# A graph network on one core: another order of the first products, their loads and waits, fewer products of a constant, and a square root moved at the end

## The reference

```python
Xw = X @ Wv + bv
sj, si = Xw @ aw[:d, 0], Xw @ aw[d:, 0]
e = leaky_relu(sj[:, None, :] + si[:, :, None] + ab[0], negative_slope=0.2)
alpha = A * exp(e);  T = alpha / (alpha.sum(-1, keepdims=True) + 1e-12)
H = X @ Wk[0] + bk[0] + (T @ X) @ Wk[1] + bk[1] + (T @ T @ X) @ Wk[2] + bk[2]
x = layernorm(x + relu(H))
x = layernorm(x + adj @ x @ w)
```

## Time and profile before

| what | value |
|---|---|
| median of 3 runs | 272.84 us (272.76 to 273.21) |
| the profiled execution's own time | 273.95 us |
| its span, from the first to the last instruction | 272.1 us |
| around the span | 1.85 us |
| TensorE matmuls (PE) busy | 266.3 us, 98% |
| VectorE (DVE) busy | 216.8 us, 80% |
| ScalarE (ACT) busy | 191.6 us, 70% |
| GpSimd (POOL) busy | 190.3 us, 70% |

### The profile page before, as it was taken

One profiled execution on the slowest core, in us unless ns is written; L12 is line 12 of the kernel. 1 busy time (PEld: TensorE's weight loads), 2 busy tenths in 40 slices (PEclk: granted clock), 3 DMA queues, 4 the chain that ended last, 5 costly groups with the idle time before them and its releaser, 6 DMA issues.

```text
span 272.1 us, 6029 instructions
## 1 busy us (share of the span) xinstructions
PE 266.3 (98%) x1887; PEld 246.6 (91%) x1887; DVE 216.8 (80%) x615; ACT 191.6 (70%) x437; POOL 190.3 (70%) x412
## 2 busy tenths in 40 slices
PE   8999999999999999999999999999999999999992
PEld 3899999999999999999999999999999999999991
DVE  0677788888898888889888888988888888788994
ACT  2688677776667777666777766677766677767874
POOL 2567547788777777877778787777887777657533
PEclk9999999999999999999999999999999999999998
DMA  7858245749584378545764448844883347922214
GB/s 222 292 164 135 30 147 125 81 139 150 150 151 145 58 136 140 165 142 155 126 86 123 146 155 143 150 121 79 133 161 99 117 115 87 135 75 77 79 41 154
DMA packets 28758, 34.91 MB, mean 128 GB/s; under 512 B 7091, under 2 KB 16694, under 8 KB 28726
## 3 DMA queue, kind: packets, MB, share of 16 engines
q1 hardware_dynamic: 28016, 34.12, 56.7%
q10 hardware_dynamic: 710, 0.40, 0.5%
HBM read 26.09 MB, written 8.42 MB: 127 GB/s over the span
## 4 chain that ended last, share of the span: by engine, by line
PE 93%; DVE 2%; DMA 1%; POOL 1%; ACT 1%; issue 1%; POOLq 0%; ACTq 0%
PE ps_v L1123 30%; PE ps_y L1123 16%; PE ps_out L1123 14%; PE ps_h L1123 11%; PE ps_agg L1300 10%; PE ps_v L1233 3%; PE ps_v L1237 3%; PE ps_v L1235 3%; PE ps_agg L1123 2%; DMA WY_sb<-Wk_dram 1%; PE ps_y L1151 1%; PE ps_v L1151 1%; POOL rstd L1025 1%; DVE stats L865 0%; DVE y L878 0%
## 5 line engine op out<-in xcount | busy, mean ns | idle before, releaser
L1123 PE MATMUL ps_v<-WX_hi,XT_hi 128*128 128x512 f32 (+1 forms) x128 | 47.7, 373 | 0.0
L1123 PE MATMUL ps_v<-WX_lo,XT_hi 128*128 128x512 f32 (+1 forms) x128 | 47.4, 371 | 0.0
L1123 PE MATMUL ps_v<-WX_hi,XT_lo 128*128 128x512 f32 (+1 forms) x128 | 47.4, 371 | 0.0
L1040 POOL TENSOR_TENSOR XT_lo<-xt,XT_hi 128x512 fp32r<-128x512 f32 x32 | 41.3, 1293 | 5.4 <-DVE WX_lo L964 2.7
L1052 POOL TENSOR_TENSOR alpha<-exps,adjs 128x256 f32<-128x256 f32 x31 | 22.9, 740 | 30.3 <-ACT exps L477 30.0
L1056 POOL TENSOR_TENSOR alpha_lo<-alpha,alpha_hi 128x256 fp32r<-128x256 f32 x31 | 22.8, 734 | 18.4 <-ACT alpha_hi L486 18.4
L509 ACT ACTIVATE y<-res,offset,rstd 128x256 f32<-128x256 f32 x62 | 33.6, 590 | 0.8 <-POOL offset L1016 0.8
L1123 PE MATMUL ps_y<-WY_hi,XT_hi 128*128 128x258 f32 x112 | 34.1, 304 | 0.0
L1300 PEld LDWEIGHTS ps_agg<-adjs,y 128*128 128x128 f32 x248 | 32.0, 191 | 2.3
L1300 PE MATMUL ps_agg<-adjs,y 128*128 128x128 f32 x248 | 32.7, 275 | 0.0
L502 ACT ACTIVATE V_hi<-ps_v 128x512 fp32r<-128x512 f32 x32 | 19.1, 597 | 19.1 <-PE ps_v L1123 18.9
(11 more groups left out here) (177 smaller groups left out, 838.7 us busy)
## 6 DMA issues: line engine op xcount, KB each, us to landing
xt<-xt_dram SPq DMA_DIRECT2D x32, 256.0 KB, 5.3
nodes<-nodes_dram SPq DMA_DIRECT2D x32, 256.0 KB, 5.4
out_dram<-out_sb SPq DMA_DIRECT2D x30, 256.0 KB, 5.0
adjs<-adjs_dram SPq DMA_DIRECT2D x32, 128.0 KB, 5.3
spread<-si_rows_dram SPq DMA_DIRECT2D x29, 128.0 KB, 4.7
W_sb<-Wk_dram SPq DMA_DIRECT2D x2, 256.0 KB, 3.9
si_rows_dram<-scores SPq DMA_DIRECT2D x29, 1.0 KB, 3.6
WY_sb<-Wk_dram ACTq DMA_DIRECT2D x1, 256.0 KB, 4.1
```

The source lines that it names most:

```text
L1040: pool.tensor_tensor(XT_lo[k % 7][:].rearrange("p c b i -> p (c b i)"), xt_sb[k % 4][:], XT_hi[k % 7][:].rearrange("p c b i -> p (c b i)") ...
L1123: last = pe.matmul(to, a, b, start=start and n == 0, stop=stop and n == 2, skip_group_check=True)
```

## The change

The order of the ramp becomes another one:

- TensorE: seven products of the constant instead of nine; then hop 0 of pair 0 on whole float32 (`first_hop0`), the score weights between its graphs; `score_shift`; the split hop 2 of pair 0 with the score columns; hop 1 of pair 0 as split products, graph 0 ahead of the transposes for pair 0 and graph 1 behind them; hop 2 of pair 1; the sum of the biases, now two fp32r products (`bk_hi`, `bk_lo`) into ps_y; T V2 of pair 0.
- Loads: Wk[0] is the first of ScalarE's queue, and Wk[2] comes behind the vectors in SyncE's, ahead of Wk[1]. SyncE no longer waits for X0 ahead of a weight. X4 moves ahead of adjacency 2, and w behind adjacency 4. SyncE's wait ahead of X4 is for hop 0 instead of hop 1.
- ScalarE: an Exp of one element right behind the first load; the parts `_hi` of Wk[0], Wk[2], Wk[1] and of the biases ahead of X1's; the scores of pair 0 from hop 2; X4's part ahead of leaky 1; in step 0 alpha_hi of pair 2 ahead of V2_hi of pair 4.
- VectorE: WY_lo in two parts (the score columns straight from PSUM), then Wk[1]'s `_lo`, then Wk[0]'s; x1 of pair 0 is copied graph by graph; `first_hop0` (x0 of pair 0) goes behind `first_v`; in step 0 the inverse of pair 1 ahead of `first_h`.
- The exps and alpha of pair 0 live in the two halves of ps_out, so that pair 1 need not wait for them.
- GpSimd: X0's `_lo` ahead of the vectors' sums; X4's ahead of alpha 1; Wk[1] is no longer waited for; alpha_lo of pair 2 ahead of the norm of pair 0.
- End: root 1 ahead of normalisation 0 of pair 30.

```diff
             load_xt(0)
             sp.dma_start(WvT_sb[:], WvT.rearrange("(c p) n -> p c n", p=P)).then_inc(WvT_loaded, DMA)
+            sp.dma_start(vectors_sb[:].rearrange("p c n -> p (c n)"), vectors).then_inc(vectors_loaded, DMA)
+            load_Wk(2)
             load_Wk(1)
-            sp.wait_ge(xt_loaded[0], DMA)
-            load_Wk(0)
             load_xt(1)
+            sp.wait_ge(Wk_loaded[0], DMA)
+            load_adjs(0)
             sp.wait_ge(Wk_loaded[2], DMA)
-            load_adjs(0)
-            sp.wait_ge(Wk_loaded[1], DMA)
             load_xt(2)
...
-            act.dma_start(WY_sb[:, :, 0:D], Wk[2].rearrange("(c p) n -> p c n", p=P)).then_inc(Wk_loaded[2], DMA)
-            act.dma_start(vectors_sb[:].rearrange("p c n -> p (c n)"), vectors).then_inc(vectors_loaded, DMA)
+            act.dma_start(W0_sb[:], Wk[0].rearrange("(c p) n -> p c n", p=P)).then_inc(Wk_loaded[0], DMA)
+            act.activation(exps[:, 0, 0:1], one, ACT.Exp)
...
             last_std2_of(0)
+            last_std2_of(1)
             late_normalise_from_psum(0)
-            last_std2_of(1)
             late_normalise_from_psum(1)
...
+            dve.wait_ge(WY_hi_ready, 1)
+            dve.tensor_tensor(WY_lo[:, :, 0:D], WY_sb[:], WY_hi[:, :, 0:D].bitcast(F32), ALU.subtract)
             dve.wait_ge(u_done, 1)
...
+            dve.tensor_copy(WY_hi[:, :, D:D + 2], ps_u).then_inc(u_ready, 1)
+            dve.wait_ge(u_ready, 1)
+            dve.tensor_tensor(WY_lo[:, :, D:D + 2], ps_u, WY_hi[:, :, D:D + 2].bitcast(F32),
+                              ALU.subtract).then_inc(WY_ready, 1)
...
                 if there(k + 2):
                     alphas(k + 2)
+                    alpha_lo_of(k + 2)
                     if k == 0:
                         norm1(0)
-                    alpha_lo_of(k + 2)
...
+            def first_hop0(b):
+
+                pe.wait_ge(xt_loaded[0], DMA)
+                pe.wait_ge(Wk_loaded[0], DMA)
                 X = xt_sb[0][:].rearrange("p (c b i) -> p c b i", c=C, b=PER)
                 for c in range(C):
-                    last = pe.matmul(to, X[:, c, b], weights[:, c], start=c == 0, stop=c == C - 1,
+                    last = pe.matmul(ps_h[:, b], X[:, c, b], W0_sb[:, c], start=b == 0 and c == 0, stop=c == C - 1,
                                      skip_group_check=True)
...
-            keep_warm(ps_v[:, 0], 9)
-            first_hop2(0)
+            keep_warm(ps_v[:, 0], 7)
+            first_hop0(0)
             score_weights()
-            first_hop2(1)
+            first_hop0(1)
+            score_shift()
+            hop2_and_scores(0)
             first_hop1(0)
-            score_shift()
-            first_hop1(1)
-            sum_of_biases()
             pe.wait_ge(identity_ready, 1)
             spread_scores(0)
-            hop0(0)
+            first_hop1(1)
             hop2_and_scores(1)
+            sum_of_biases()
             pe.wait_ge(ones_columns_ready, 1)
             propagate_v2(0)
```

More of the change, by code:

```diff
@@ L396, in step @@
                     load_adjs(k + 3)
-                if there(k + 9) and k >= -5:
+                if there(k + 9) and k >= -4:
                     load_xt(k + 9)
@@ L400, in step @@
                     load_adjs(4)
+                    sp.dma_start(w_sb[:], w.rearrange("(c p) n -> p c n", p=P)).then_inc(w_loaded, DMA)
                 if there(k - 3):
                     store(k - 3)
-            for k in range(-5, LAST + 2):
+            for k in range(-4, LAST + 2):
                 step(k)
@@ L431, in wx_hi, with bk_hi_of, wy_hi @@
                 act.wait_ge(Wk_loaded[n], DMA)
-                act.activation(WX_hi[:, :, 1 - n], (W0_sb, W1_sb)[n][:, :, 0:D], ACT.Copy).then_inc(WX_hi_ready[n], 1)
+                act.activation(WX_hi[:, :, 1 - n], (W0_sb, W1_sb)[n][:], ACT.Copy).then_inc(WX_hi_ready[n], 1)
+            def bk_hi_of():
+                act.wait_ge(bk_loaded, DMA)
+                act.activation(bk_hi[:], bk_sb[:], ACT.Copy).then_inc(bk_hi_ready, 1)
+            def wy_hi():
+                act.wait_ge(Wk_loaded[2], DMA)
+                act.activation(WY_hi[:, :, 0:D], WY_sb[:], ACT.Copy).then_inc(WY_hi_ready, 1)
             def scores_of(k):
                 act.wait_ge(y_done, k + 1)
+                if k == 0:
+                    act.wait_ge(shift_ready, 1)
                 act.activation(scores[k % 3][:].rearrange("p n b -> p b n"), hop2(k)[:, :, D:D + 2], ACT.Identity,
                                bias=shift[:]).then_inc(scores_ready, 1)
[L439 to L451, removed]
             def v2_hi(k):
@@ L472, in exponentials @@
                 act.wait_ge(leaky_ready, k + 1)
-                if k == 1:
-                    act.wait_ge(first_alpha_ready, 1)
                 if k > 1:
                     act.wait_ge(alpha_ready, k - 1)
-                act.activation(exps[:], leaky[:], ACT.Exp).then_inc(exp_ready, 1)
+                act.activation(exps[:] if k > 0 else first_exps, leaky[:], ACT.Exp).then_inc(exp_ready, 1)
             def alpha_hi_of(k):
@@ L485, in alpha_hi_of @@
                     act.wait_ge(av1_done, k - 1)
-                act.activation(alpha_hi[k % 2][:], alpha[:], ACT.Copy).then_inc(alpha_hi_ready, 1)
+                act.activation(alpha_hi[k % 2][:], alpha[:] if k > 0 else first_alphas,
+                               ACT.Copy).then_inc(alpha_hi_ready, 1)
             def scale_v(k):
@@ L697, in first_alpha, with first_hop1 @@
                 dve.wait_ge(adjs_loaded[0], DMA)
[L698 removed]
+                dve.tensor_tensor(first_alphas, first_exps, adjs_sb[0][:], ALU.mult).then_inc(first_alpha_ready, 1)
             def first_alpha_lo():
                 dve.wait_ge(alpha_hi_ready, 1)
[L702 removed]
+                dve.tensor_tensor(alpha_lo[0][:], first_alphas, alpha_hi[0][:].bitcast(F32),
                                   ALU.subtract).then_inc(first_alpha_lo_ready, 1)
[L705 to L709, removed]
+            def first_hop1(b):
+                dve.wait_ge(*((first_half_done, 1) if b == 0 else (v1_done, 1)))
+                dve.tensor_copy(first_x1[:, b], ps_v[:, b, 0:D]).then_inc(first_x1_ready, 1)
             def first_v():
                 dve.wait_ge(inv_ready, 1)
[L713 removed]
+                dve.wait_ge(first_x1_ready, PER)
                 for b in range(PER):
@@ L773, in v1_lo @@
                                   ALU.subtract).then_inc(v1_lo_ready, 1)
[L775 to L782, removed]
             def v2_lo(k):
@@ L916, in step @@
                     return
+                if k > 0 and not both_hops(k):
+                    scale_h(k)
+                inverse(k + 1)
                 if k == 0:
                     first_h()
-                elif not both_hops(k):
-                    scale_h(k)
-                inverse(k + 1)
                 if both_hops(k):
```

137 lines of the change are left out of this document (61 added, 76 removed).

## The result

The changed kernel takes 274.60 us (median of 22 executions, 272.88 to 276.48) where the kernel before takes 272.99 (22 executions, 272.76 to 273.84). The ratio of the two is 1.0052, with an interval of 1.0031 to 1.0073: slower by half a per cent.

A forecast was written before the change was run, and what follows sets the result against it. TensorE's own work was taken to bound the kernel (93% of the chain). Terms -0.31 - 0.22 - 0.25 + 0.10 - 0.11 = -0.79 us took 272.84 to 272.05 us; range 271.5 to 273.8.

The forecast's parts named there:

- Zero, if the clock rises as before: Start of the ramp: Wk[0] replaces Wk[2] at the head of ScalarE's queue, no gain or loss until 8.70.
- the first rival: Ramp: TensorE's 1.07 us idle makes the clock rise later, price 1.1 to 1.9 us, 273.75 us in all; chance 0.28.
- TensorE starts at 4.94 again: Start: the first useful product begins at 4.94 as before, since the first load lands no earlier.
- Just hidden; the cover is 0.1 to 0.6 us: Hop 2 of pair 0: split Wk[2] lets it start at 8.2 to 8.7, TensorE wants it at 8.82.
- The second rival: Hop 2 of pair 0: with an earlier clock rise it waits for split Wk[2]; -0.2 in all, 272.65 us; chance 0.22.
- I take as it is: The shown runs' median lies 1.11 us below the profiled execution; the forecast difference of -0.79 is applied to 272.84 unchanged.
- The alpha chain: Transposes to T V2 of pair 0: keeps 3.23 us, starts 0.31 earlier, TensorE waits some 0.5; gain 0.31 us.
- The waits behind: GpSimd waits before hop 2 of pair 4 and T V2 of pair 2 go: -0.22 and -0.25 us.
- The part given back: ScalarE scales V1 of pair 2 later, behind the later norm of pair 0: +0.10 us, bounds 0 and 0.3.
- The end: Root 1 ahead of normalisation 0 lets SyncE's third store go at 269.6 instead of 269.7: -0.11 us, bound 0.4.

The follow-up runs named there:

- the run with seven late ones: Kernel before with seven products instead of nine, started 0.8 us later by waiting for GpSimd's identity: 273.39 us, ratio 1.0004, two of 12 over 274.5.
- the run with the filled gaps: Changed kernel, seven products, plus three products ahead of the score weights and one ahead of hop 2 of pair 0: 274.36 us, ratio 1.0052 to the kernel before.

## Why the prediction was wrong

**The step that failed: the start, "Zero, if the clock rises as before".** The condition doesn't hold with seven products: it cost 2.3 us by the medians in the kernel before, and in the changed kernel the seven cost 1.6 us, since nine bring it level. It was the first rival, and it was given 0.28. The runs with 7, 8, 9 and 10 products in an otherwise unchanged kernel show that a shorter fill alone makes long executions, and the run with seven late ones that it is mostly the gap that does it. "TensorE starts at 4.94 again" didn't hold either: the first weight landed 3.3 to 3.8 us after its issue instead of 3.9 to 4.25. With seven products this made the gap shorter (0.23, 0.62 and 0.71 us in three traces, 0.91 in the kernel before), which may be why half of the changed kernel's executions are long and not three quarters. Why the load landed earlier isn't known. The prediction held that no row shows what a gap of 1 us does; that was so, and it should have weighed the one short gap in the rows as the reason for nine, not as a curiosity.

**The price of that rival was too low.** I let the lower pace end with the shift, so 1.1 to 1.9 us, and took 1.7. In the long execution with seven products, the transposes of pair 0 start at 13.80; in the profile with ten they start at 10.50: 3.3 us, twice my value. The clock stayed low until about 12, through both graphs of hop 2 and one of hop 1 too. The middle group of that kernel, near 274.8, fits 1.7 us by its time, though no trace shows it; the other has twice that. So also the forecast by one number failed in form: the change made a mixture, and the median of a mixture depends on where the heaps' shares stand. At eleven of 22, it fell between them.

**The second step that failed: "Just hidden; the cover is 0.1 to 0.6 us".** The second rival held, in the short executions. With an early rise the kernel before starts T V2 of pair 0 at 13.75 (ten products), the changed order at 14.25 (nine). The chain of waits with ten, 4 to 16 us:

```profile
5.14 0.98 PE ps_y L1151 x4
6.12 0.82 PE ps_out L1329 x8
...
10.50 0.36 PE ps_out L1215 x2
...
13.75 0.29 PE ps_v L1233
```

and that of the changed kernel with nine, 3 to 16 us:

```profile
2.12 5.01 DMA WY_sb<-Wk_dram
...
7.16 0.64 ACT WY_hi L445
...
7.82 0.69 DVE WY_lo L675
...
8.84 1.74 PE ps_y L1113 x12
...
11.29 0.22 PE ps_out L1193 x2
...
14.25 0.36 PE ps_v L1210
```

The first needs only raw weights until the transposes, so a fast clock helps it. The second waits for Wk[2]. I had set its landing at 6.4 to 6.9 us; it landed at 7.31 in the profile of the changed kernel, at 7.13 with nine products, and at 6.73 in the run with the filled gaps. Transposes at 11.29 instead of 10.50: the work saved, 0.31 us, is more than lost. The spans of these two traces, 271.6 and 271.3 us, put the changed order 0.2 us behind, where the rival had it 0.2 us ahead; the medians of the executions don't tell the two apart. I had read the ramp from an execution whose clock rose late: its first four records took 2.00 us, and 1.50, 1.32 and 1.18 in the three other traces with nine products in that order; and it was 1.11 us over the median. That execution flattered the changed order. The difference that "I take as it is" was partly the very quantity that the change acts on.

**The alpha chain bounds, but it is shorter than was said.** The 3.23 us of the earlier trace rows are TensorE's own work between the transposes and T V2 of pair 0 (0.36 + 1.44 + 1.43), and TensorE didn't wait there; I had taken them for the length of the chain. From the transposes to T V2 it is 2.96 us in both profiles of the changed order, and there TensorE did wait for it, 0.17 us by the chain (its own work ended at 14.21). I had said 0.5: the chain is 0.27 shorter, the two products of the biases took 0.43 with their change of operand instead of 0.24, and the transposes 0.22 instead of 0.36.

**The waits behind were right.** -0.22 became -0.20 (1.66 to 1.46), and T V2 of pair 2's wait went, 0.27 us for 0.25. I had read it in the wrong row: T V1 of pair 1 takes 0.95 us in the changed kernel as it took 0.96, and the wait stood in front of and in the first product of T V2, 25.74 to 26.13 in the chain, where the changed kernel has 0.12. The part given back, where ScalarE scales V1 of pair 2, was expected at 0.1: the twelve products of pair 2 take 2.90 instead of 2.80 in the chain.

```profile
28.27 2.90 PE ps_v L1113 x12
```

**The end gained nothing.** Root 1 goes ahead, and SyncE's three stores follow each other, as was said:

```profile
267.47 0.29 ACT L559 ACTIVATE last_std<-last_moments,epsilon 128x1 f32<-128x1 f32 x1 [0.15 <-DVE last_moments L884]
...
268.25 0.33 SPq L413 DMA_DIRECT2D out_dram<-out_sb  x1
268.62 0.92 SPq L416 DMA_DIRECT2D out_dram<-last_out_sb  x2
```

From the start of TensorE's last product to the start of SyncE's third store it took 2.79 us before and 2.72 after, by the timelines: 0.07, expected 0.11. But the third store's issue takes 0.45 instead of 0.35, and the last two stores land 2.1 us after their issue instead of 1.9. From the same product's start to the end of the span it is 5.25 us before and 5.34 after; the six traces with the old end have 5.21 to 5.26, the two of the kernel before with the new end 5.25 and 5.26, the six of the changed order 5.33 to 5.35. So the term of -0.11 is nothing, or a loss of up to 0.1.

The middle steps cost the same in both kernels: from the end of pair 2's products (31.70 before, 31.17 after) to the start of the last product (266.89 and 266.37) it is 235.2 us in both. So all but the end was decided in the first 32 us.

**What stays open.** What exactly decides, in one execution, whether the rise comes early or late: the same kernel with seven products has all three groups. The traces show the pace, not the reason, and the level of the clock is read from the pace alone: the granted clock is recorded as 1.00 up to 12 us in the long execution with seven products too. The part of WvT's lateness in the long executions of the run with Wk[2] ahead of WvT wasn't tried alone.

## What to carry to other kernels

Where TensorE works ahead of its first useful product only to raise its clock, the fill should reach to that product: look at the latest landing and the idle time in front of it, not at the sum of the fill. Look at all executions, not at the median: a kernel that loses its clock in five of 12 has an unchanged median (eight products: 273.16) and a long tail. Before a ramp's steps are summed from one trace, ask at which pace that execution ran and what would bind if the pace doubled; a step that needs loads which have landed gains from a fast clock, one that waits for a load and its split doesn't.

## What the runs showed of the hardware

Kernels whose gap between the constant products and the first useful one was 0.91 us in the profile had nine executions of 12 that were 1.7 or 3.4 us longer; with 0.65 us it was five of 12, with 0.18 us one of 128. A gap is not enough for a late rise in one execution: 0.71 us stood before a first graph of 1.10 us, 0.62 before one of 2.04. The moment of the rise differs between executions: near 6.8 us in the profile of before, ahead of the first four records with ten products (0.98 us instead of 2.00), near 12 us in the long ones. By the Trainium skill ("TensorE: Matmul & The Clock Gate", "What's actually happening") the moment isn't tied to the kernel's start; the spread of the executions agrees.

A load's landing moves from trace to trace and with the order: the 256 KB at the head of ScalarE's queue took 3.9 to 4.25 us in the eight traces with Wk[2] there, and 3.3 to 3.8 in the six with Wk[0] there. The 3 KB of vectors took 4.1 to 4.7 us from second place in ScalarE's queue, and 3.5, 3.8 and 4.9 us from third place in SyncE's in three traces of one order.

VectorE's subtraction of two operands in SBUF took 1.15 us instead of 0.41 while GpSimd ran a 1.29 us subtraction. The Trainium skill ("SBUF — State Buffer", "SBUF: two separate sides") says that the two engines share one pair of ports, and that whoever starts first holds it for the whole instruction; this row agrees, and so does the 0.42 us of the same subtraction with one operand in PSUM beside a GpSimd subtraction of 1.28 us. GpSimd's wait for Wk[1]'s split, which looked needless in the kernel before, had kept the two apart: there X3's part starts at 15.55, after alpha_lo's end at 14.21, and not at 12.46.
